# The last block's stages as single-engine pieces in a written-out order, with GpSimd's four scatters ahead of its four gathers

## What is computed

```python
fused = sig * dense_output + (1.0 - sig) * sparse_output
x = _layernorm(src + fused, ln1_g, ln1_b)
ff = jax.nn.relu(x @ ff1_w.T + ff1_b) @ ff2_w.T + ff2_b
return _layernorm(x + ff, ln2_g, ln2_b)
...
x = x + ga * _L1_attn_ref(h, ...)
h = _layernorm(x, axis=-1) * (1 + cb) + sb
x = x + gb * _L1_ffn_ref(h, ...)
```

## Time and profile before

| what | value |
|---|---|
| median of 3 runs | 1895.65 us (1894.76 to 1895.8) |
| the profiled execution, its time | 1893.34 us |
| the profiled execution, its span | 1891.3 us |
| busy shares of the span | TensorE 71%, VectorE 62%, ScalarE 50%, GpSimd 17% |
| granted TensorE clock, mean | 0.863 of full |
| the last block | 1492.4 us to the end, 21% of the span |

### The profile page before, as it was taken

The page is one execution under the profiler, slowest core; times in us unless marked ns, Lnnn a source line. Parts: engine busy times, 40 slices in busy tenths (PEclk is TensorE's granted clock), DMA queues, the critical chain, the costliest instruction groups (busy, mean ns, idle before and its releaser), DMA issues. The chain is left out here.

```text
span 1891.3 us, 27295 instructions
## 1 busy us (share of the span) xinstructions
PE 1348.0 (71%) x8229; PEld 795.3 (42%) x8308; DVE 1170.9 (62%) x3214; ACT 944.1 (50%) x1330; POOL 317.6 (17%) x358
## 2 busy tenths in 40 slices
PE   4577742999906541899999999998999453575772
PEld 3355532899903320233333333333333432464662
DVE  2655563566665750888888888888888324334342
ACT  3233310343403331888888888888887133344331
POOL 0000013663341103000000000000000003032474
PEclk9888865999957875999999999999999676687886
DMA  6600000333302323222222212222220300011142
GB/s 189 195 0 0 0 11 22 104 112 93 89 25 75 113 65 46 36 38 34 33 35 34 33 35 33 33 38 35 33 34 4 109 12 28 26 37 32 44 116 71
DMA packets 115839, 99.43 MB, mean 53 GB/s; under 512 B 10818, under 2 KB 93216, under 8 KB 115680
## 3 DMA queue, kind: packets, MB, share of 16 engines
q1 hardware_dynamic: 100064, 77.62, 18.0%
q0 software_dynamic: 8192, 16.79, 3.2%
q10 hardware_dynamic: 7472, 3.66, 0.7%
HBM read 55.69 MB, written 42.34 MB: 52 GB/s over the span
## 5 line engine op out<-in xcount | busy, mean ns | idle before, releaser
L1793 ACT ACTIVATE probs<-scores_ps 128x1024 f32<-128x1024 f32 x512 | 508.3, 1026 | 152.7 <-PE scores_ps L1813 147.2
L1813 PE MATMUL scores_ps<-q_pack,k_pack 128*128 128x512 bf16 x946 | 279.4, 384 | 84.3 <-DMA q_pack<-shift_pieces_dram 50.7
L1830 PE MATMUL pv_ps<-probs,v_pad 128*32 128x512 f32 x2048 | 273.5, 606 | 1.1 <-ACT probs L1793 1.1
L1984 DVE TENSOR_SCALAR_CACHE_REDUCE junk<-sparse_scores,at 128x1024 f32<-128x1024 f32 x192 | 245.6, 1279 | 6.9
L1813 PEld LDWEIGHTS scores_ps<-q_pack,k_pack 128*128 128x128 bf16 x1024 | 72.9, 98 | 363.8 <-ACT probs L1793 172.1
L1743 POOL COPY v_pad<-v 128x256 f32 x16 | 6.2, 399 | 637.5 <-PE pv_ps L1830 637.3
L1127 ACT ACTIVATE hidden_experts<-pre_experts 128x512 f32<-128x512 f32 x94 | 59.3, 631 | 106.0 <-DVE pre_experts L1086 66.9
L1149 PE MATMUL up_ps_experts<-x_t_experts,up_weights_now_experts 128*128 128x128 f32 x752 | 103.5, 282 | 0.8 <-ACT x_t_experts L1120 0.7
L1086 DVE TENSOR_TENSOR pre_experts<-up_ps_experts,weights_t 128x512 f32<-128x512 f32 x94 | 64.6, 687 | 55.4 <-PE up_ps_experts L1149 55.4
L1156 PE MATMUL down_ps_experts<-weights_t,hidden_experts 128*128 x736 | 97.2, 275 | 0.0
L1149 PEld LDWEIGHTS up_ps_experts<-x_t_experts,up_weights_now_experts 128*128 128x128 f32 x752 | 92.9, 195 | 3.0 <-ACT x_t_experts L1120 1.1
(11 more groups left out here) (370 smaller groups left out, 2443.3 us busy)
## 6 DMA issues: line engine op xcount, KB each, us to landing
q_pack<-q_pieces_dram SPq DMA_DIRECT2D x144, 64.0 KB
k_pack<-k_pieces_dram SPq DMA_DIRECT2D x144, 64.0 KB
expert_rows_dram<-zeros SPq DMA_DIRECT2D x1, 6400.0 KB, 21.3
x_rows_experts<-expert_rows_dram SPq DMA_DIRECT2D x25, 256.0 KB
expert_rows_dram<-y_rows_experts SPq DMA_DIRECT2D x46, 128.0 KB
q_pieces_dram<-q_pieces SPq DMA_DIRECT2D x12, 256.0 KB, 2.4
k_pieces_dram<-k_pieces SPq DMA_DIRECT2D x12, 256.0 KB, 2.6
expert_rows_dram<-zeros SPq DMA_DIRECT2D x1, 2560.0 KB, 28.2
```

Source lines behind the costliest of these rows:

```text
L1793: act.activation(probs[:, kt % 2, j, :], scores_ps[n % 2][:], ACT.Exp, scale=SCALE1).then_inc(exp_done, 1)
L1813: ins = pe.matmul(scores_ps[n % 2][:, c * 512 : c * 512 + 512], k_pack[:, group % 2, j, kt * P : kt * P + P], q_pack[:, group % 2, j, c * ...
L1830: ins = pe.matmul(pv_ps[32 * j : 32 * j + 32, c, :], v_pad[:, group % 2, kt, j, :], probs[:, kt % 2, j, c * 512 : c * 512 + 512], start=(k ...
L1984: step(dve.tensor_scalar(junk[:], s[:, t, :], at[:, t : t + 1], None, ALU.is_ge, ALU.add, accum_out=count[:, t : t + 1]))
```

## The change

`in_stages` is gone. A string, `TAIL_ORDER`, lists 518 pieces of work, each of them `name.half`, `name.half.part`, `name.batch` or `name.batch.expert.part`. A new function `walk` goes through it on every engine and calls what that engine has for the name. What was one stage on several engines has a name for each: `dense` (TensorE), `attended` (VectorE), `root1` (ScalarE), `invert1` (VectorE), `norm1` (ScalarE), and so on; `ff_up`, its relus, `go_up` and the transposes are split by part too. `send` is GpSimd's scatter, `pick` its gather.

```diff
+TAIL_ORDER = """
+turn_ctx.0 turn_ctx.1 keep_ctx.0 keep_ctx.1 dense.0 dense.1 attended.0 turn_ctx.2 turn_ctx.3 keep_ctx.2 root1.0 dense.2 keep_ctx.3 invert1.0
...
+go_up.2.7.1 relu.2.7.0 combine.0 go_down.2.6 relu.2.7.1 turn_x.3.0 turn_x.3.1 keep_x.3.0 keep_x.3.1 turn_x.3.2 keep_x.3.2 bias.2.6 store.0 go_up.3.0.0
...
+def walk(order, stages):
+
+    for stage in order.split():
+        name, *at = stage.split(".")
+        if name in stages:
+            stages[name](*map(int, at))
...
+HS = 4
...
-        hs = a.sb("src_and_sparse", [P, 2, HT, C])
+        hs = a.sb("src_and_sparse", [P, HS, HT, C])
...
-                def load(b):
+                def load_x(b):
...
+                def send(b):
                     pool.wait_ge(send_ready, b + 1)
                     pool.wait_ge(n_ready[2], 2 * b + 2)
...
+                def pick(b):
+                    pool.wait_ge(pick_ready, b + 1)
+                    pool.wait_ge(y_stored[b], 16)
+                    if b >= 3:
+                        pool.wait_ge(combined, 2 * (b - 3) + 2)
...
+                walk(TAIL_ORDER, dict(send=send, pick=pick))
...
+                def invert1(u):
+                    if u >= 2:
+                        dve.wait_ge(n_ready[0], u - 1)
                     invert(0, u)
...
-                def relu(b, e):
-                    if e % 2 == 1:
...
                 def norm1(u):
                     if u >= 2:
                         act.wait_ge(turn_made, turns.number("n1", u - 2))
+                        act.wait_ge(yb_ready, u - 1)
...
-                for u in range(2):
+                for u in range(HS):
                     load(u)
```

More of the change, by code:

```diff
@@ new lines @@
+ff_down.3 invert3.1 keep_n1.5 attended.6 norm3.1 update.2 root1.6 ff_up.4.1 ff_relu.4.0 turn_n3.1 ff_relu.4.1 ff_up.4.2 keep_n3.1 ff_out.3 ff_up.4.3
+root3.2 ff_relu.4.2 logits.1 ff_relu.4.3 ff_up.5.0 best.0 root2.3 ff_down.4 invert3.2 invert2.3 norm3.2 pos.0 y_bias.5 ff_up.5.1 norm2.3 index.0
+turn_n3.2 turn_ctx.7 keep_n3.2 update.3 send.0 ff_relu.5.0 logits.2 ff_relu.5.1 ff_up.5.2 keep_ctx.7 ff_up.5.3 ff_relu.5.2 invert1.6 root3.3 dense.7
+ff_relu.5.3 invert3.3 norm1.6 ff_out.4 norm3.3 turn_n1.6 attended.7 ff_down.5 root2.4 keep_n1.6 invert2.4 root1.7 y_bias.6 norm2.4 turn_n3.3 invert1.7
@@ L2611, in _ @@
                 sp.dma_start(down_w[:], dram["L1_ffn_W2"].rearrange("e (k p) c -> p (e k) c", p=P)).then_inc(weights_loaded, 16)
[L2612 to L2613 removed]
+                walk(TAIL_ORDER, dict(load_x=load_x, store_y=store_y, store=store))
                 sp.wait_ge(out_stored, 16 * HALVES)
@@ L2820, in combine @@
                         ins.then_inc(combined, 1)
-                in_stages(
-                    dense=dense, norm1=norm1, ff_up=ff_up, ff_down=ff_down, norm2=norm2, norm3=norm3, best=best, places=places, expert=expert, gates=gates, combine=combine
+                for b in range(B):
+                    step(dve.tensor_tensor(gain[:, b, :], g.row("L1_attn_ln2_g"), g.mods[1][:, b, GA * C : GA * C + C], ALU.mult))
+                step(dve.tensor_tensor(y_bias[:], g.row("L1_attn_ln1_b"), g.row("L1_attn_ff2_b"), ALU.add))
+                dve.wait_ge(cols_made, 1)
+                dve.tensor_copy(cols[:], small_ps[:, COLS_AT : COLS_AT + COLS]).then_inc(cols_ready, 1)
+                step.settle()
+                walk(
+                    TAIL_ORDER,
+                    dict(
+                        attended=attended,
+                        invert1=invert1,
+                        y_bias=add_y_bias,
+                        ff_out=ff_out,
+                        invert2=invert2,
+                        update=update,
+                        invert3=invert3,
+                        best=best,
+                        index=index,
+                        bias=bias,
+                        keep_y=keep_y,
+                        gates=gates,
+                        combine=combine,
+                    ),
                 )
@@ new lines, in go_up @@
+                def go_up(b, e, pair):
+                    if b == 0 and e == 0:
+                        pe.wait_ge(weights_loaded, 32)
+                    for n in range(len(TURN_PARTS)):
+                        turned("x", b, n)
+                    key = ("expert", b, e, pair)
+                    slot = ups.at(*key)
+                    after(pe, up_free[slot], ups.emptied_before(*key))
+                    for i in range(2):
+                        k = 2 * pair + i
+                        ins = pe.matmul(
+                            up_ps[slot][:, i * 256 : i * 256 + CAPACITY], up_w[:, e, k * P : k * P + P], x_t[:, e * CAPACITY : (e + 1) * CAPACITY], start=True, stop=True
+                        )
+                    ins.then_inc(up_made, 1)
```

462 lines of the change are left out of this document (192 added, 270 removed).

## The result

The kernel after takes 1736.18 us (median of 4 runs, 1735.43 to 1736.98), the kernel before 1895.2 us (4 runs, 1894.38 to 1895.8): a ratio of 0.9161, 95% interval 0.9145 to 0.9177. The profiled execution has a span of 1734.0 us. It is almost the floor of rival 3, 1732 us.

What follows compares the result with a forecast made beforehand. It took poorly interlocked engines to bound the kernel up to 1793.35 and GpSimd's DMAs after; with `send.3` at 1649 (terms one and two) plus 109.6 the span was 1758.6, forecast 1763 us, range 1740 to 1802.

Steps and rivals of the forecast that it cites:

- rival 3: From its first scatter on, GpSimd is the only bound, with utilisation 1 before it: 1732 us, the floor; chance 0.08.
- first term: Start to first scatter: 59 us of work at utilisation 0.70 from 1498.3, so the scatter at 1583, against 1585.1 before.
- Second term: `send.0` to `send.3`: 66 us, GpSimd's 60.6 with slips at utilisation 0.87, so `send.3` starts at 1649.
- Third term: `send.3` to the end: 109.6 us against 97.95 before, if the gathers never wait for stored rows.
- What was costed at nothing: Extra load issues of four-deep source rows, new semaphore waits and relus moved to ScalarE were taken to add no time.
- the cover argument: Expert blocks: moved relus take ScalarE 1.25 us per expert, covered by TensorE's 2.17; uncovered they would cost 10 us.
- Above the span: Allowance from span to median: span 1758.6 us gave 1763, as the median before stood 4.35 us above the span.
- 1, a clock of 0.75: TensorE stays at a mean clock of 0.75 up to `send.3`, which starts at 1673: 1787 us; chance 0.22.
- 2, expert blocks bind: Expert blocks, not GpSimd, bind after `send.3`, 26.4 us from store to store: 121.8 us for 109.6, 1775 us; chance 0.10.
- 4, slower DMA issues: GpSimd's DMA issues slow beside a fuller VectorE, 0.08 more for each of 128, 10 us: 1773 us; chance 0.05.
- 5, no overlap: Halves don't overlap, `send.3` stays at 1793, the gather of batch 0 costs its 11.7 us: 1907 us; chance 0.03.

Runs made afterwards that it cites:

- half_gathers_3: Kernel after without the gathers of each token's second row, the sums taking the first row twice, on an undisturbed chip: 1718.3 us.
- old_order_new_pieces: Kernel after with its pieces listed in the order of the kernel before: 1894.47 us, ratio 0.9993 to the kernel before.
- hs2: Kernel after with two buffers of source rows for four, on a disturbed chip: 1947.35 us, first scatter 68.34 us after GpSimd's memset.
- relu_split: Kernel after with the relu of an odd expert's second pair given back to VectorE: 1740.3 us, ratio 0.9182 to the kernel before.
- pool_order_alone: Kernel before with only GpSimd's list changed, to four scatter groups and then four gathers: 1919.34 us, ratio 1.0125.
- pick0_before_send3: Kernel after with the gather of batch 0 moved ahead of the scatters of batch 3: 1752.86 us, ratio 0.9248 to the kernel before.
- after_again: Kernel after, unchanged, as its job's baseline on a disturbed chip: 1951.13 us, ratio 0.9345 to the kernel before.
- after_3: Kernel after, unchanged, run again in the last job: 1735.84 us.

## Why the prediction was wrong, step by step

**The failed step: the utilisation in the first term, 0.70.** The text put it so: "because every piece still needs a handoff and the first 16 us have one half to work on". Measured is 59.6 / 63.0 = 0.95 for TensorE: handoffs cost it next to nothing, since another half's piece was ready each time (all its waits in this window come to 2.5 us). The first scatter came at 1561.2 for 1583: 21.8 of the 24.6 us by which the span was missed. The reason given for 0.70 does not hold: the list has `dense` of halves 0 to 3 ahead of the first `turn_n1`, and in the first 16.8 us TensorE is busy 14.75 already:

```profile
1498.20:1515.00 16.80, 14.75 (x77) 11.72 (x77) 8.97 (x41) 9.69 (x20) 0.00 (x0) 0.80 0.92 275
```

The value was taken halfway between the old utilisation of 0.49 and 1, though the profile had a row for mixed work, 14.46 of 16 us busy at clock 1.00, which is 0.90; 1498.3 + 59 / 0.90 = 1563.9 would have been within 3 us. That row was used for the second term (with 0.87 for its 0.90) and not for the first. The sizes under it were mixed: TensorE's 58 us was right (59.6). VectorE's 59, which counts the gaps between instructions, was too much: it was busy 50.0 and waited 9.5 of the 63, so it took some 53.5 with its gaps.

**Second term, 66 us from `send.0` to `send.3`:** measured 1624.2 - 1561.2 = 63.0. GpSimd's own list was the bound: 62.0 us for 48 scatters where 60.6 was taken, and one wait of 0.98. The utilisation of 0.87 was not needed, since VectorE's and TensorE's work for the next batches ran ahead. 3 us too long.

**Third term, 109.6 us from `send.3` to the end:** measured 1734.0 - 1624.2 = 109.8. Right, with its condition: the last store of rows goes out 73.2 us behind `send.3`, where 75 was worked out from `combine.1` in VectorE's way, and lands before the gathers at + 80.7 need it. The margin was named as about one microsecond and is near three. `half_gathers_3` shows what stands behind it: with 30 us less of gathers ahead of the last group, GpSimd waits for these rows.

**What was costed at nothing** (four-deep source rows, more semaphores, relus on ScalarE) was nothing, as `old_order_new_pieces` shows, and `hs2` for the first scatter; with the new order the relus are worth 4 us (`relu_split`), which the cover argument had not seen, since it looked at ScalarE and not at what VectorE gets rid of.

**Above the span** I added 4.35 us for the median; it was 2.2. That is 2 of the 27 us.

**Rivals.** 1, a clock of 0.75: no, 0.95 to 0.97 in all three stretches. (The constants ahead of them ran at 0.50 again, with TensorE busy 5.05 of 5.8 us.) 2, expert blocks bind: no, but they are the next bound (of 30 us of gathers taken away ahead of the last group, 8 come through). 3, GpSimd the only bound: this is what happened, 1736 for its 1732; I gave it 0.08. 4, slower DMA issues: 1.28 us each over 128, where 1.25 was taken; 4 us over the list at most. 5, no overlap: its price, 11.7 us for the gather of batch 0 behind the last scatters, was too low: `pool_order_alone` gave 24, since the late gather delays the stores too. The case itself did not arise.

## What to carry to other kernels

Where a list of pieces keeps several units of work in flight, size the first stretch by the utilisation that the profile shows where work is already mixed (here 14.5 of 16 us), not by a middle value between the old one and 1. An order that puts a serial queue's late work behind its early work pays only if the producers of the early work are sped up with it: alone it cost 24 us here; with the rest it is part of a gain of 159, and putting one gather back ahead of the last scatters costs 17 (`pick0_before_send3`). For a queue that then runs without gaps the time is the sum of its idle times, so an earlier first start is worth nothing if the next group isn't ready.

## What the hardware showed that was not expected

On the two disturbed chips whole engines paused where the other chips show no pause. The lines of the up matmuls of the first layer's experts (busy and mean ns, then the idle time before them with what ended it), first of the kernel after on its chip, then of the same kernel in `after_again`:

```profile
L1149 PE MATMUL up_ps_experts<-x_t_experts,up_weights_now_experts 128*128 128x128 f32 x752 | 103.9, 282 | 0.8 <-ACT x_t_experts L1120 0.7
```

```profile
L1149 PE MATMUL up_ps_experts<-x_t_experts,up_weights_now_experts 128*128 128x128 f32 x752 | 113.2, 299 | 82.9 <-issue 49.4 <-DVE up_weights_now_experts L1081 15.5 <-ACT hidden_experts L1127 11.5
```

The waits of the last block there. The first row is GpSimd's wait for row numbers (69.0 us in 2 waits on the undisturbed chip); in the others the releaser is not an instruction of another engine but "remote" or "issue", with single pauses of 9 to 17 us:

```profile
POOL expert_rows_dram L2581 <- DVE send_to_tail L2717: 110.9, 4, 68.1
ACT hidden_tail L2889 <- remote: 67.5, 11, 12.4
DVE expert_out_t_tail L2728 <- remote: 64.4, 7, 16.5
...
PEld down_ps_tail L3025 <- issue: 37.1, 12, 9.4
```

The attention part took the same on both: ScalarE's exponentials 508.6 us in one trace and 508.4 in the other, TensorE's products with the values 272.7 and 274.6. The first scatter of the kernel after came 68.0 or 68.1 us after the memset on every chip. A matmul of L1149 takes 275 ns in the median of both traces. So the matmuls and the copies are no slower there, they start late, and in some stretches only.

The stretches have one thing in common. In the last block of `after_again` VectorE and ScalarE have 14 pauses of over 4 us that the profile marks "remote"; each begins while GpSimd is issuing one of its groups of 16 indirect DMAs, and none ends later than 3.4 us behind the group. In the first layer's experts there are 21 more, and each of them begins inside such a group too. Up to the first scatter, and in the attention part, GpSimd issues no group, and there is no such pause. With half the gathers the pause shown above ends 15.9 us behind the store of batch 0's rows, where it ended 25.1 us behind it with all of them. In the traces of `after` and `after_3` the same groups go out with no such pause beside them. Why the groups stop the other engines on two chips and not on the others was not tried; no run moved a group away to see. The order's gain is 8.4% where there are none (0.9158 and 0.9161) and 6.6% where there are (0.9345), since GpSimd then waits 8.8 to 20.2 us ahead of each group behind the first.
